# Loads of x and of the adjacency issued by ScalarE in place of SyncE, in a kernel of two graph attention layers and a multi-head attention

## The chip, the core and the metric

The kernel runs on one core of a Trainium2 chip. The metric is the device time of one execution in microseconds. SyncE (SP in the profile) has no arithmetic: here it issues all DMAs. ScalarE is ACT, VectorE DVE, GpSimd POOL, TensorE PE.

## The reference

64 independent graphs, each of 128 nodes with 256 features (float32) and an adjacency of 128 x 128 (int32). Two residual blocks are applied, each behind a layer norm and a relu:

```python
h = maximum(layernorm(x), 0)
x = x + gat(h)        # two graph attention layers
h = maximum(layernorm(x), 0)
x = x + mha(h)        # 8 heads of 32, masked by adj

def gat_layer(x, mask, W, a_src, a_dst, bias):   # H=4,F=128, elu; then H=1,F=256
    xl = (x @ W).reshape(B, N, H, F)
    e = leaky_relu(asrc[:, :, None, :] + adst[:, None, :, :], 0.2)
    attn = softmax(where(mask, e, -1e9), axis=1)
    return einsum('bsdh,bshf->bdhf', attn, xl) + bias
# mha: softmax(q k / sqrt(32), masked) v, relu, @ Wo
```

## The kernel before

All work is a software pipeline over the graphs, one graph per step. In step t, the function at lag (phase) p works on graph t - p; lags go from 0 (load of x) to 11 (store), so there are 75 steps. Each engine has a list of pairs (function, phase), written out by hand, which it runs in this order in each step. Engines meet only through semaphores: `done(eng, sem, g)` waits for a graph's result, `free(eng, sem, g, ring)` for a buffer's earlier user, and tiles have rings of 2, 4 or 8 buffers.

TensorE's list begins a step with mha's masks and scores (graph t-8) and goes on with scores of the attention layers, project_out (the output projection, L815 with attT), aggregate1, project_v and qk (L815 with h2T), aggregate2 (L929), project2 (L840) and mha_av. It ends the step with project1 (L815 with hT), which needs the transposed, normed x of graph t-3.

Matrices are multiplied in float16 halves (a high part and a remainder). The halves of h, h2, att and of the exponentials e3 are transposed by DMA: SyncE issues `dma_start_transpose` for them. SyncE's list in a step is: e3_transpose_last (phase 9, L257), att_transpose (10, L276), store of the result (11, L252), norm1_transpose (3, L263, gives hT), e3_transpose_first (8, L257), load_adj (1, L248), load_x (0, L242), norm2_transpose (6, L270, gives h2T). The first x tiles, the first adjacency and the weights are issued ahead of the steps. x_in has 8 buffers, adj_in 4. load_x waits for x1_set of graph n-8, load_adj for masks_set of graph n-4. x is first read two steps after its load (norm1_moments, VectorE), the adjacency likewise (masks, GpSimd).

ScalarE's list is relevant around mha's exponentials (phase 8, L497, four heads in each half): mha_exp_first, then elu_exp (L460), gat2_copy (L477), mha_exp_last, qk_copy (L487), gat1_exp (L448), relu2 (L482). Nothing else than ACTIVATEs is in its list. VectorE gives nmx3 (negated row maxima, L761) that the exponentials need, and gat1_recip (L752) reads the sums of gat1_exp.

Of the kernel before, what the change touches and what calls it, by code (L numbers as in the profile page):

```python
# [51 lines left out]
def wait(eng, sem, value):  # L52

    if value > 0:
        eng.wait_ge(sem, value)


def done(eng, sem, g):

    wait(eng, sem, g.n + 1)  # L60


def free(eng, sem, g, ring=2):

    wait(eng, sem, g.n + 1 - ring)
# [13 lines left out]
def gnn_kernel(nc, x, adj, W1, att_src1, att_dst1, b1, W2, att_src2, att_dst2, b2, Wq, Wk, Wv, Wo, out):  # L79
# [9 lines left out]
    with ctx:  # L89
        def sb(name, shape, dt=F32):  # L90
            return ctx.enter_context(nc.sbuf_tensor(name, shape, dt))

        def sem(name):
            return ctx.enter_context(nc.semaphore(name))
# [34 lines left out]
        x_in = sb("x_in", [128, 8, D])  # L129
        adj_in = sb("adj_in", [128, 4, N], I32)  # L130
# [72 lines left out]
        s = {n: sem(n) for n in names}  # L203
        x_here = [sem(f"x_here{i}") for i in range(8)]
        adj_here = [sem(f"adj_here{i}") for i in range(4)]
# [10 lines left out]
        def steps(body, before=None):  # L216

            def step(t):  # L220
                body([Graph(t - lag, G) for lag in range(LAGS)])

            for t in range(G + LAGS - 1):
                if before and t in before:
                    before[t]()
                step(t)

        def run(body_functions, graphs):
            for function, phase in body_functions:
                if graphs[phase].active:  # L230
                    function(graphs[phase])
# [3 lines left out]

        @block.sync
        def _(sp):
            def load_x(g):
                if g.n < 3:
                    return  # L240
                free(sp, s["x1_set"], g, 8)
                sp.dma_start(x_in[:, g.eight, :], x[g.n]).then_inc(x_here[g.eight], 16)  # L242

            def load_adj(g):
                if g.n == 0:
                    return
                free(sp, s["masks_set"], g, 4)
                sp.dma_start(adj_in[:, g.four, :], adj[g.n]).then_inc(adj_here[g.four], 16)  # L248

            def store(g):  # L250
                done(sp, s["x_out_set"], g)
                sp.dma_start(out[g.n], x_out[:, g.four, :]).then_inc(stored[g.four], 16)  # L252

            def e3_transpose(g, half, low_set):
                done(sp, s[low_set], g)
                free(sp, s["av_done"], g)
                sp.dma_start_transpose(e3T[:, g.two, half].rearrange("p s h n -> p (s h) n"),  # L257
                                       e3_split[:, g.two, half].rearrange("p s h n -> p (s h n)")).then_inc(e3T_here[2 * half + g.two], 16)

            def norm1_transpose(g):  # L260
                done(sp, s["hT_set"], g)
                free(sp, s["xl_done"], g)
                sp.dma_start_transpose(hT[:, g.two].rearrange("p s (k n) -> p (s k) n", n=N),  # L263
                                       h_split[:, g.two].rearrange("p s c -> p (s c)")).then_inc(hT_here[g.two], 16)

            def norm2_transpose(g):
                done(sp, s["h2T_set"], g)
                free(sp, s["qk_done"], g)
                free(sp, s["v_done"], g)
                sp.dma_start_transpose(h2T[:, g.two].rearrange("p s (k n) -> p (s k) n", n=N),  # L270
                                       h2_split[:, g.two].rearrange("p s c -> p (s c)")).then_inc(h2T_here[g.two], 16)

            def att_transpose(g):
                done(sp, s["attT_set"], g)
                free(sp, s["wo_done"], g)
                sp.dma_start_transpose(attT[:, g.two].rearrange("p s (k n) -> p (s k) n", n=N),  # L276
                                       att_split[:, g.two].rearrange("p s c -> p (s c)")).then_inc(attT_here[g.two], 16)

            def e3_transpose_first(g):
                e3_transpose(g, 0, "e3_low_first")  # L280

            def e3_transpose_last(g):
                e3_transpose(g, 1, "e3_low_last")

            for n in range(2):
                sp.dma_start(x_in[:, n, :], x[n]).then_inc(x_here[n], 16)
            for k in range(KD):
                sp.dma_start(w1[:, k, :, 0:HF // 2], W1[k * 128:(k + 1) * 128, :].rearrange("p (a c) -> p a c", a=2)).then_inc(s["w1_in"], 16)
            for k in range(2):
                sp.dma_start(att1[:, k, :], (att_src1, att_dst1)[k].rearrange("h f -> (h f)").partition_broadcast(128)).then_inc(s["w1_in"], 16)  # L290
            sp.dma_start(b1_all[:, :], b1.partition_broadcast(128)).then_inc(s["w1_in"], 16)
            sp.dma_start(x_in[:, 2, :], x[2]).then_inc(x_here[2], 16)
            sp.dma_start(adj_in[:, 0, :], adj[0]).then_inc(adj_here[0], 16)
            sp.dma_start(w2[:, :, 0:D], W2.rearrange("(k p) n -> p k n", p=128)).then_inc(s["w2_in"], 16)
            for k in range(2):
                sp.dma_start(att2[:, k, :], (att_src2, att_dst2)[k].rearrange("h f -> (h f)").partition_broadcast(128)).then_inc(s["w2_in"], 16)
            sp.dma_start(b2_all[:, :], b2.partition_broadcast(128)).then_inc(s["w2_in"], 16)
            for m, W in enumerate((Wq, Wk, Wv, Wo)):
                sp.dma_start(proj[:, :, m, :], W.rearrange("(k p) n -> p k n", p=128)).then_inc(s["proj_in"], 16)

            steps(lambda graphs: run([
                (e3_transpose_last, 9), (att_transpose, 10), (store, 11), (norm1_transpose, 3), (e3_transpose_first, 8),
                (load_adj, 1), (load_x, 0), (norm2_transpose, 6),
            ], graphs))

            for n in range(4):
                sp.wait_ge(stored[n], 16 * (G // 4))
# [106 lines left out]
        def _(act):  # L414
            def split_high(m):
# [2 lines left out]
                act.activation(proj_split[:, 0, :, m, :], proj[:, :, m, :], ACT.Copy, scale=scale[:, 2 + m:3 + m]).then_inc(s["split_high"], 1)  # L418
                act.activation(proj[:, :, m, :], proj[:, :, m, :], ACT.Copy, scale=scale[:, 2 + m:3 + m]).then_inc(s["w_scaled"], 1)

            def relu1(g):
                done(act, s["z_set"], g)
                wait(act, hT_here[g.two], g.dma2 - 16)
                act.activation(h_split[:, g.two, 0, :], z[:, g.two, 0, :], ACT.Relu).then_inc(s["hT_high"], 1)  # L424
# [88 lines left out]
            def att_copy(g):  # L513
# [3 lines left out]

            steps(lambda graphs: run([
                (v_copy, 9), (relu1, 3), (gat2_leaky, 6), (att_copy, 10), (abT_copy, 4), (gat1_copy, 5), (gat2_exp, 6),
                (gat1_leaky, 4), (mha_exp_first, 8), (elu_exp, 5), (gat2_copy, 6), (mha_exp_last, 8), (qk_copy, 7),  # L520
                (gat1_exp, 4), (relu2, 6),
            ], graphs), before={5: lambda: (split_high(0), split_high(1)), 6: lambda: split_high(2), 7: lambda: split_high(3)})

# [495 lines left out]
```

## Time and profile before

| | us |
|---|---|
| median of 3 runs (773.32 to 776.01) | 775.59 |
| the profiled execution | 774.69 |
| its span | 772.6 |
| TensorE busy | 716.3 |
| VectorE busy | 681.4 |
| ScalarE busy | 591.6 |
| GpSimd busy | 515.8 |

The span runs from the first to the last instruction of the profiled execution. Busy times are sums over an engine's instructions. DMA issues don't count as busy for the engine that makes them; they appear in timelines as rows of its queue (SPq is SyncE's), and their duration is that of the issue, not of the transfer. A transfer's time to landing counts from the issue's start. An idle time is put down to what ended it.

### The profile page before, as it was taken

How to read it: one execution, taken by the hardware profiler on the slowest of the kernel's cores; microseconds unless marked ns; L12 is line 12 of the kernel's file. 1: busy time of each engine (PE TensorE's matmuls, PEld its weight loads, DVE VectorE, ACT ScalarE, POOL GpSimd, SP SyncE). 2: the span in 40 equal slices, each digit the busy share in tenths (PEclk: the TensorE clock that was granted, in tenths of full speed). 3: DMA queues.
4: the chain of work that ended last, by engine and by line, in shares of the span. 5: the costliest groups of instructions: out<-in, count | busy, mean ns of one | idle time of the engine just before them, and what ended most of it. 6: DMA issues, size and time to landing. Idle time of an engine off the chain costs nothing.

```text
span 772.6 us, 26496 instructions
## 1 busy us (share of the span) xinstructions
PE 716.3 (93%) x8398; PEld 593.4 (77%) x8398; DVE 681.4 (88%) x2017; ACT 591.6 (77%) x1865; POOL 515.8 (67%) x733
## 2 busy tenths in 40 slices
PE   0389999999999999999999999999999999999973
PEld 0157788888888888888888888888888888788852
DVE  4758899999999999999999999999999989999873
ACT  0167888888888778888888788788888888788752
POOL 5456777676767676667667766676677767766551
PEclk9999999999999999999999999999999999999996
DMA  6111555666578566557766656766655666655464
GB/s 197 33 37 43 106 112 112 121 110 118 118 117 115 116 112 113 119 114 115 122 110 118 112 124 115 115 110 120 114 119 116 113 119 106 112 118 105 89 110 89
DMA packets 270423, 84.70 MB, mean 110 GB/s; under 512 B 242896, under 2 KB 269904, under 8 KB 270288
## 3 DMA queue, kind: packets, MB, share of 16 engines
q1 hardware_dynamic: 270288, 83.02, 57.8%
q8 instruction: 70, 1.15, 0.7%
q14 instruction: 65, 0.53, 0.3%
HBM read 15.86 MB, written 8.39 MB: 31 GB/s over the span
## 4 chain that ended last, share of the span: by engine, by line
PE 75%; DVE 9%; DMA 5%; issue 4%; SPq 3%; ACT 1%; POOL 1%; DVEq 0%; ACTq 0%; POOLq 0%
PE bank L815 28%; PE bank L840 11%; PE bank L986 7%; PE bank L947 6%; DMA hT<-h_split 4%; PE bank L966 3%; PE bank L929 3%; PE bank L936 3%; PE bank L866 3%; PE bank L891 2%; PE bank L889 2%; PE bank L881 2%; SPq L276 1%; DVE top L756 1%; PE bank L874 1%
## 5 line engine op out<-in xcount | busy, mean ns | idle before, releaser
L497 ACT ACTIVATE e<-bank,nmx,q_power 128x128 f32<-128x128 f32 x512 | 194.7, 481 | 5.1 <-DVE nmx L761 5.1
L372 POOL CAST e_split<-e 128x512 f16<-128x512 f32 x128 | 82.4, 643 | 118.6 <-ACT e L497 118.6
L374 POOL TENSOR_TENSOR e_split<-e,e_split 128x512 f16<-128x512 f32 x128 | 151.7, 1185 | 10.3
L840 PE MATMUL bank<-w,h1T 128*128 128x258 f32 x512 | 122.8, 382 | 0.7 <-DVE shift L599 0.7
L386 POOL TENSOR_TENSOR rstd<-var,minus_half 128x1 f32<-128x1 f32 x128 | 71.7, 560 | 66.6 <-DVE var L625 66.6
L815 PE MATMUL bank<-w_split,hT 128*128 128x260 f16 x768 | 98.2, 278 | 12.3 <-DMA hT<-h_split 11.9
L840 PEld LDWEIGHTS bank<-w,h1T 128*128 128x128 f32 x512 | 96.6, 190 | 16.6 <-DVE h1T L655 1.6
L448 ACT ACTIVATE eT<-lr,nmx 128x128 f32<-128x128 f32 x256 | 102.7, 458 | 0.8 <-DVE nmx L713 0.8
L815 PE MATMUL bank<-h2T,proj_split 128*128 128x128 f16 x1536 | 97.4, 220 | 1.6 <-DMA h2T<-h_split 1.6
L815 PEld LDWEIGHTS bank<-h2T,proj_split 128*128 128x128 f16 x1536 | 92.0, 99 | 3.7 <-DMA h2T<-h_split 2.4
L815 PEld LDWEIGHTS bank<-w_split,hT 128*128 128x128 f16 x768 | 71.1, 98 | 24.5 <-issue 7.0
L364 POOL TENSOR_TENSOR eTn<-eT,rs 128x512 f32<-128x512 f32 x64 | 67.0, 1046 | 17.9 <-DVE rs L752 17.9
L756 DVE TENSOR_REDUCE top<-bank 128x8 f32<-128x1024 f32 x64 | 77.3, 1208 | 0.3 <-PE bank L947 0.3
L424 ACT ACTIVATE h_split<-z 128x256 f16<-128x256 f32 x64 | 26.6, 416 | 65.9 <-DVE z L631 65.9
L947 PEld LDWEIGHTS bank<-qkT 32*128 32x128 f16 x1536 | 43.0, 93 | 37.7 <-issue 36.0
L986 PE MATMUL bank<-en,xl 128*128 128x128 f32 x512 | 68.3, 276 | 0.2
L448 ACT ACTIVATION_READ_ACCUMULATOR eT<-lr,nmx 128x1 f32 x256 | 65.7, 257 | 0.0
L947 PE MATMUL bank<-qkT 32*128 32x128 f16 x1536 | 64.8, 216 | 0.3 <-DVE qkT L724 0.2
L986 PEld LDWEIGHTS bank<-en,xl 128*128 128x128 f32 x512 | 62.2, 192 | 2.0 <-ACT en L455 1.3
L604 DVE SCALAR_TENSOR_TENSOR h_split<-z,h_split 128x256 f16<-128x256 f32 x128 | 61.5, 481 | 0.6 <-ACT h_split L424 0.5
L815 PE MATMUL bank<-proj_split,attT 128*128 128x256 f16 x384 | 54.3, 279 | 6.1 <-DMA attT<-att_split 6.1
L440 ACT ACTIVATE lr<-bank,ab 128x128 f32<-128x128 f32 x64 | 23.5, 368 | 43.6 <-PE bank L867 43.6
(116 smaller groups left out, 1921.7 us busy)
## 6 DMA issues: line engine op xcount, KB each, us to landing
x_in<-in_x_dram SPq DMA_DIRECT2D x64, 128.0 KB, 2.3
out_dram<-x_out SPq DMA_DIRECT2D x64, 128.0 KB, 2.0
adj_in<-in_adj_dram SPq DMA_DIRECT2D x64, 64.0 KB, 2.5
e3T<-e_split SPq DMA_TRANSPOSE x128, 3.1
hT<-h_split SPq DMA_TRANSPOSE x64, 2.4
h2T<-h_split SPq DMA_TRANSPOSE x64, 2.5
attT<-att_split SPq DMA_TRANSPOSE x64, 2.8
w<-in_L_gnn_W_dram SPq DMA_DIRECT2D x2, 256.0 KB, 3.1
```

Source lines behind the costliest of these rows:

```text
L364: pool.tensor_tensor(eTn[:, g.two, :].rearrange("p (h n) -> p h n", h=H), eT[:, g.two, :].rearrange("p (h n) -> p h n", h=H), rs[:, g.two, ...
L372: pool.tensor_copy(e3_split[:, g.two, half, 0], e).then_inc(s[high_set], 1)
L374: pool.tensor_tensor(e3_split[:, g.two, half, 1], e, e3_split[:, g.two, half, 0], ALU.subtract).then_inc(s[low_set], 1)
L386: pool.tensor_tensor(rstd[:, g.two, which:which + 1], var[:, g.two, which:which + 1], minus_half[:, :], ALU.pow).then_inc(s[rstd_set], 1)
L448: ins = act.activation(eT[:, g.two, h * N:(h + 1) * N], lr[:, g.two, h * N:(h + 1) * N], ACT.Exp, bias=nmx[:, g.two, h:h + 1], accum_out=s ...
L497: ins = act.activation(e3[:, g.two, h, :], S[:, h // 4, (h % 4) * N:(h % 4 + 1) * N], ACT.Exp, bias=nmx3[:, g.two, h:h + 1], scale=q_power ...
L604: dve.scalar_tensor_tensor(out=out_, in0=in_, scalar=0.0, in1=high_, op0=ALU.max, op1=ALU.subtract).then_inc(s[sem_], 1)
L756: dve.tensor_reduce(top3[:, g.two, :], S.rearrange("p b (h n) -> p (b h) n", h=4), AX.X, ALU.max, negate=True).then_inc(s["top3_set"], 1)
L815: ins = pe.matmul(out_, left, right, start=n == 0, stop=n == len(pairs) - 1)
L840: ins = pe.matmul(X2[:, 0:D + 2], h1T[:, g.two, k * F:(k + 1) * F], w2[:, k, :], start=k == 0, stop=k == H - 1)
L947: ins = pe.matmul(S[:, b, col * N:(col + 1) * N], qkT[r, g.two, i, h // 4, :], qkT[r, g.two, j, 2 + h // 4, :], start=False, stop=n == 2 a ...
L986: ins = pe.matmul(O1[:, h * N:(h + 1) * N], xl[:, g.two, h * F:(h + 1) * F], en[:, g.two, h * N:(h + 1) * N], start=True, stop=True)
```

## The change

load_x and load_adj move from SyncE's block to ScalarE's, with the same waits and semaphores. In ScalarE's list load_x stands behind mha_exp_first, and load_adj behind mha_exp_last. SyncE's list loses both. The loads ahead of the steps stay on SyncE.

```diff
@@ SyncE
             steps(lambda graphs: run([
                 (e3_transpose_last, 9), (att_transpose, 10), (store, 11), (norm1_transpose, 3), (e3_transpose_first, 8),
-                (load_adj, 1), (load_x, 0), (norm2_transpose, 6),
+                (norm2_transpose, 6),
             ], graphs))
@@ ScalarE
+            def load_x(g):
+                if g.n < 3:
+                    return
+                free(act, s["x1_set"], g, 8)
+                act.dma_start(x_in[:, g.eight, :], x[g.n]).then_inc(x_here[g.eight], 16)
+
+            def load_adj(g):
+                if g.n == 0:
+                    return
+                free(act, s["masks_set"], g, 4)
+                act.dma_start(adj_in[:, g.four, :], adj[g.n]).then_inc(adj_here[g.four], 16)
...
-                (gat1_leaky, 4), (mha_exp_first, 8), (elu_exp, 5), (gat2_copy, 6), (mha_exp_last, 8), (qk_copy, 7),
+                (gat1_leaky, 4), (mha_exp_first, 8), (load_x, 0), (elu_exp, 5), (gat2_copy, 6), (mha_exp_last, 8), (load_adj, 1), (qk_copy, 7),
                 (gat1_exp, 4), (relu2, 6),
```

## Rows read from the trace of the kernel before

**Rows 1.** The page: busy us (share of the span) and instructions of an engine.
```profile
PE 716.3 (93%) x8398; PEld 593.4 (77%) x8398; DVE 681.4 (88%) x2017; ACT 591.6 (77%) x1865; POOL 515.8 (67%) x733
```
**Rows 2.** Windows: stretch, then busy us (count) of PE, PEld, DVE, ACT, POOL, clock, DMA.
```profile
100.00:700.00 600.00, 596.30 (x7146) 500.63 (x7145) 562.32 (x1691) 497.96 (x1579) 423.50 (x601) 1.00 0.64 115
```
**Rows 3.** The chain of waits, its longest pieces: start us, length us, what.
```profile
93.66 2.00 PE bank L815 x30
...
203.28 2.00 PE bank L815 x30
...
214.14 2.00 PE bank L815 x30
...
709.88 2.00 PE bank L815 x30
```
**Rows 4.** Waits of the whole span: waiter, releaser, us in total, times, longest us.
```profile
DVE x L738 <- PE bank L929: 23.8, 59, 1.8
...
PE bank L815 <- DMA hT<-h_split: 11.9, 9, 7.0
```
**Rows 5.** Timeline of SyncE's queue, one undisturbed step: start us, length us, instruction.
```profile
202.87 1.19 SPq L276 DMA_TRANSPOSE attT<-att_split  x1
204.11 0.57 SPq L252 DMA_DIRECT2D out_dram<-x_out  x1
204.77 1.19 SPq L263 DMA_TRANSPOSE hT<-h_split  x1
...
207.37 0.57 SPq L248 DMA_DIRECT2D adj_in<-in_adj_dram  x1
207.99 0.44 SPq L242 DMA_DIRECT2D x_in<-in_x_dram  x1
210.46 1.20 SPq L270 DMA_TRANSPOSE h2T<-h_split  x1
```
**Rows 6.** Waits of SyncE's queue before an issue.
```profile
SPq L270 <- DVE h_split L604: 111.6, 64, 5.2
```
**Rows 7.** Timeline of ScalarE in the same step; the last row ends gat1_exp.
```profile
202.55 1.50 ACT L497 ACTIVATE e<-bank,nmx,q_power 128x128 f32<-128x128 f32 x4
...
203.93 0.70 ACT L460 ACTIVATE ex<-bank,minus_one 128x512 f32<-128x512 f32 x1
...
204.66 1.54 ACT L497 ACTIVATE e<-bank,nmx,q_power 128x128 f32<-128x128 f32 x4
...
207.96 0.25 ACT L448 ACTIVATION_READ_ACCUMULATOR eT<-lr,nmx 128x1 f32 x1
```
**Rows 8.** Timeline of VectorE: nmx3, gat1_recip, and nmx3 of the next step.
```profile
202.19 0.32 DVE L761 TENSOR_SCALAR nmx<-top,q_power 128x8 f32<-128x8 f32 x1
...
208.24 0.18 DVE L752 RECIPROCAL rs<-sm 128x4 f32<-128x4 f32 x1
...
212.93 0.32 DVE L761 TENSOR_SCALAR nmx<-top,q_power 128x8 f32<-128x8 f32 x1
```
**Rows 9.** The page's DMA issues: count, size, median us to landing.
```profile
x_in<-in_x_dram SPq DMA_DIRECT2D x64, 128.0 KB, 2.3
...
hT<-h_split SPq DMA_TRANSPOSE x64, 2.4
```
**Rows 10.** Timeline of TensorE in the same step: aggregate2 and project1.
```profile
205.11 0.65 PE L929 MATMUL bank<-xl,en 128*128 128x256 f32 x2
...
207.95 1.49 PE L815 MATMUL bank<-w_split,hT 128*128 128x260 f16 x12
```
**Rows 11.** Timeline of SyncE's queue: first and last long store, a long norm1 transpose.
```profile
138.38 1.50 SPq L252 DMA_DIRECT2D out_dram<-x_out  x1
...
248.23 2.17 SPq L263 DMA_TRANSPOSE hT<-h_split  x1
...
666.45 1.68 SPq L252 DMA_DIRECT2D out_dram<-x_out  x1
```

More of the change, by code:

```diff
@@ L237, in _ @@
         def _(sp):
[L238 to L248, printed above, removed]
             def store(g):
```

## The prediction

> **What bounds the kernel now.** I read the page's engine totals first [rows 1]: TensorE shows 716.3 us of busy time in the 772.6 us span, VectorE 681.4, ScalarE 591.6. The middle of the run is tighter than that: in the 600 us from 100 to 700, TensorE is busy 596.3, VectorE 562.3, ScalarE 498.0, at full granted clock [rows 2]. A matmul's end is modelled, so I don't take 99% as proof; the chain of waits gives a step's length. From the first to the last of its 56 middle steps (93.66 to 709.88) a step takes 11.00 us, and an undisturbed one 10.86 (203.28 to 214.14) [rows 3]. The chain in between is matmuls with no waits. So what is not TensorE's own work in the middle is (11.00 - 10.86) x 56 = 8 us. The list of waits names where it is lost: the wait for hT, SyncE's norm1 transpose, which project1 needs: 11.9 us in 9 waits, one of 7.0 among them [rows 4].
>
> **The part taken from SyncE.** Per step it loses a load of the adjacency (0.57 us) and one of x (0.44), back to back; with the gaps that is 1.06 us of a queue of 11 us [rows 5]. What stands behind them is norm2's transpose. It starts at 210.46, and the loads ended at 208.43: the queue stood empty for 2.0 us, and it waited for VectorE before all 64 of these transposes, 111.6 us in total [rows 6]. So this removal is worth nothing: norm2's transpose waits for the same h2_split as before, and what is late next is unchanged. The transposes and stores that feed project1 (att transpose at 202.87, store 204.11, norm1 transpose 204.77) come before the loads in a step; the wait of 2.0 us cuts them off from the loads of the step before. The removal can't shorten that part.
>
> **The part given to ScalarE.** 61 loads of x and 63 of the adjacency. Both free() waits are met two steps earlier (x1 of graph n-8, masks of graph n-4), so they hold nothing. The first loads may go out earlier in the ramp, before SyncE's queue of weights is through; nothing waits for them there, and I take 0. What matters is the time that the issue takes from ScalarE, and no row shows an issue on it. Bounds: nothing, if its sequencer has handed over the four exponentials and issues the load while they run (1.50 and 1.54 us [rows 7], longer than 0.44 or 0.57); the whole 1.01 us a step, if the engine stands still.
>
> What would a microsecond on ScalarE cost? The first exponentials of mha start at 202.55, as nmx3 is ready (VectorE L761 ends at 202.51 [rows 8]), then ScalarE runs without a gap through ex (203.93), the last exponentials (204.66), qk_copy and gat1_exp, which ends at 208.21 [rows 7]. VectorE's reciprocal starts at 208.24, and it runs without a gap to the next nmx3, ended at 213.25 [rows 8]. This is a loop through two engines: 213.25 - 202.51 = 10.74 us, with both loads inside its ScalarE half. Against the mean step of 11.00 it has 0.26 us to spare. Exposure below 0.26 costs nothing; all above it is paid in each of 56 steps. I take exposure near zero, since the cover is three times the issue, and keep the other end as a rival.
>
> **What the two queues do to each other.** I also have to place the moved issues on SyncE's clock. With the exponentials handed over, the x load is issued at about 202.6 to 203.1, while SyncE issues the att transpose (202.87, 1.19 us). The adjacency load comes at about 204.2 to 205, while SyncE issues the store (204.11) and norm1's transpose (204.77) [rows 5]. Today the loads stand alone. If two issues can't overlap, one of them is late: SyncE by 0 to 1.01 us a step, between independent queues and both loads in front. I take 0.57: the adjacency falls on the store or the norm1 transpose every time, while the x load is asked for before the att transpose or behind it. A gain is excluded here, since SyncE issues the same three things.
>
> The Trainium skill, page "Perfetto Trace Analysis", section "DMA Instruction — HWDGE (DVE, Sync)", speaks against this change: one descriptor generator is shared by the two issuing sequencers, and an issue's recorded time includes the wait for its lock. "DMA: Bandwidth & Descriptors", section "Issuing engines are not separate DMA queues", sees a saving of issue time alone. By the first, ScalarE's records would come out at up to one SyncE issue longer than 0.57; by independent queues, they stay at 0.43 and 0.57 and my sum is zero. No row of before has two issuers, so the trace settles neither.
>
> What is 0.57 us worth? In an undisturbed step norm1's transpose starts at 204.77 and lands 2.4 later [rows 9], at 207.2; project1 starts at 207.95 [rows 10]: 0.75 us to spare, more than 0.57. But some steps have none: 18 stores of the 56 steps, from 138.38 to 666.45, took 1.0 to 1.8 us in place of 0.57, and 2 norm1 transposes took over 2.0 [rows 11]. That extra microsecond eats the 0.75. In these 20 steps the delay reaches project1, and it returns in the step after next, since aggregate2, whose result VectorE waits for [rows 4], stands before project1 in a step (205.11 against 207.95 [rows 10]). One delay of 0.57 is thus spread over two steps, 0.29 each: 20 x 0.29 = 5.8 us.
>
> Traffic: the x load (2.3 us to landing [rows 9]) now moves beside the att transpose, the adjacency beside norm1's. A quarter microsecond on hT's landing disappears in the 0.75, and is 20 x 0.12 = 2.4 us in the disturbed steps; I leave it in the range.
>
> **Sum**, against the profiled execution's own 774.69 us (span 772.6 and 2.1 around it): 774.7 + 0 (SyncE freed) + 0 (exposure) + 5.8 = 780.5. This execution lies 0.9 below the median of the runs, 775.59; on that scale 781.4, say 781.
>
> **Rivals.**
> (a) All hidden, nothing changes. For it: ScalarE's instructions start within 0.04 us of their releaser (202.51 to 202.55), so they wait ready; the cover is 1.5 us; the freed queue time was idle. Against: the moved issues fall on the busiest stretch of SyncE. Time 775.6, give or take 3.
> (b) Faster. The mechanism: SyncE's stream is shorter, and the long issues [rows 11], which come about once a step and drift along it, fall elsewhere than on the store. Without any loss to hT the steps are 10.86: 774.7 - 8 + 0.9 = 768. For it: two thirds of the steps already run so. Against: no load stands in front of the store. It decides if the number of long stores drops below about 10.
> (c) ScalarE stands still while it issues. Exposure of all 1.01: the loop is 10.74 + 1.01 = 11.75, so 0.75 x 56 = 42 us, 817; with half of it (0.5) 11.24, 13 us, 789. It decides from an exposure of 0.26 us. For it: the loop has next to no gap. Against: the cover. The long issues are part of this: one of 1.5 to 1.9 us behind exponentials of 1.5 shows some tenths in a few steps.
>
> **How the numbers follow.** Forecast (issues contend, 776 to 792) 0.36; (a) 0.30; (b) 0.19; (c) 0.15. The forecast's low end is a third of its price, 2 us; its high end is both loads on SyncE's part every step, 0.5 x 20 + (1.01 - 0.75)/2 x 36 = 15 us. About 0.5% (3.9 us) is what a measurement can tell from no change. Slower: all of (c) and nine tenths of the forecast, 0.47. Same: the rest of the forecast and nearly all of (a), 0.33. Faster: 0.20. The range for 8 in 10 goes down to (b), 768, and up through the forecast into the half-exposed (c), 800. The forecast's own range is 776 to 792.
>
> **What the new profile would show.** Right: loads at ScalarE's queue with issues clearly over 0.57 us, or SyncE's store and norm1 transpose longer or later by about half a microsecond; ScalarE's gap between exponentials and ex under 0.1 us; TensorE's waits for hT grown by about 6 us; SyncE's wait before norm2's transpose up by about 1 us a step, to some 170 us. Wrong: load issues at 0.43 and 0.57 with no gap behind them (then (a)); fewer long stores and a mean step near 10.86 ((b)); VectorE waiting for eT or for ex by more than 0.3 us a step, and a step of over 11.3 us ((c)). The prediction fails altogether if a ramp step's loads arrive late and norm1_moments waits for x.

## The result, and the profile after

The changed kernel takes 776.91 us (median of 22 runs, 775.29 to 781.02), the kernel before in the same comparison 774.48 (22 runs). The ratio is 1.0039, with a 95% interval of 1.0027 to 1.0051: slower by 0.4%, some 2.4 to 3 us. The direction is that of the forecast; the forecast's 781 asked for more than twice as much.

The profiled execution took 775.29 us, its span is 773.5. It is the quickest of the 22, so its span, 0.9 us over that of before, does not show the whole loss. First the page of the changed kernel, the issues with their median us to landing.

```profile
out_dram<-x_out SPq DMA_DIRECT2D x64, 128.0 KB, 2.6
x_in<-in_x_dram ACTq DMA_DIRECT2D x61, 128.0 KB, 2.5
adj_in<-in_adj_dram ACTq DMA_DIRECT2D x63, 64.0 KB, 2.8
...
hT<-h_split SPq DMA_TRANSPOSE x64, 2.5
...
attT<-att_split SPq DMA_TRANSPOSE x64, 3.5
```

The same two rows on the page of the kernel before, for the store and the att transpose:

```profile
out_dram<-x_out SPq DMA_DIRECT2D x64, 128.0 KB, 2.0
...
attT<-att_split SPq DMA_TRANSPOSE x64, 2.8
```

The DMAs that SyncE issues beside the moved loads land later, the att transpose by 0.7 us and the store by 0.6; hT by 0.1 in the median against [rows 9]. Now the waits of the changed kernel, of TensorE and of SyncE's queue, to be read against [rows 4] and [rows 6] (us in total, times, longest us):

```profile
PE bank L815 <- DMA hT<-h_split: 13.1, 10, 7.0
```
```profile
SPq L258 <- DVE h_split L604: 186.8, 64, 6.3
```

SyncE now waits 75 us longer before norm2's transpose, 1.17 a step: the freed 1.06 us turned into waiting. TensorE waits 1.2 us longer for hT. The issues themselves, in the timeline of ACT, its queue and SyncE's in one step (start us, length us, instruction):

```profile
203.29 0.33 ACTq L413 DMA_DIRECT2D x_in<-in_x_dram  x1
203.34 1.50 ACT L497 ACTIVATE e<-bank,nmx,q_power 128x128 f32<-128x128 f32 x4
...
203.60 1.19 SPq L264 DMA_TRANSPOSE attT<-att_split  x1
...
204.38 0.33 ACTq L419 DMA_DIRECT2D adj_in<-in_adj_dram  x1
...
204.70 0.71 ACT L460 ACTIVATE ex<-bank,minus_one 128x512 f32<-128x512 f32 x1
...
204.84 0.57 SPq L240 DMA_DIRECT2D out_dram<-x_out  x1
...
205.43 1.55 ACT L497 ACTIVATE e<-bank,nmx,q_power 128x128 f32<-128x128 f32 x4
```

The reader is to see three things. The four exponentials still take 1.50 us and ex still follows within their tail, so nothing of an issue is exposed (no ScalarE time stands still for it). The adjacency is issued at 204.38, 1.05 us before the exponentials that stand ahead of it in the list start: the sequencer runs ahead. And this issue lies wholly inside SyncE's issue of the att transpose (203.60 to 204.79); the transpose has its usual length, and the load's 0.33 us is that of an undisturbed issue there, as the run with the late loads shows below.

### The profile page after: what moved, and what is told of

It is laid out like the page before. It is cut to its first block, busy times and chain, and to the rows that moved or that the text cites. A ratio compares the mean times of both kernels' runs of the same rounds, so it can differ in the third digit from the quotient of the medians.

```text
span 773.5 us, 26496 instructions
## 1 busy us (share of the span) xinstructions
PE 714.1 (92%) x8398; PEld 592.0 (77%) x8398; DVE 681.2 (88%) x2017; ACT 590.8 (76%) x1865; POOL 515.0 (67%) x733
## 4 chain that ended last, share of the span: by engine, by line
PE 72%; DVE 10%; DMA 6%; issue 4%; SPq 3%; ACT 3%; POOL 1%; DVEq 0%; POOLq 0%; ACTq 0%
PE bank L815 27%; PE bank L840 10%; PE bank L986 6%; PE bank L947 6%; DMA hT<-h_split 4%; PE bank L966 3%; PE bank L929 3%; PE bank L936 3%; PE bank L866 3%; DVE top L756 2%; PE bank L891 1%; PE bank L889 1%; PE bank L881 1%; SPq L264 1%; ACT e L497 1%
```

## The experiments

Ratios are to the kernel before as it was timed in the same comparison. There were three: its median was 774.06 us beside the two runs on the start and the first two reorderings, 775.00 beside the halves, the late loads and the doubled load, and 773.83 beside the small loads and the last two reorderings. The changed kernel itself was timed in none of the three, so it is compared with them through its own ratio, 1.0039. The edits are shown shortened.

**The start.** In the profiles the second graph's project1 starts at 38.45 us after against 37.58 before (the first graph's at 26.85 against 26.00). The first three loads now go out among the weights; they were put back on SyncE, and in the mirror image they alone were moved.

```diff
+ SyncE:   (load_adj, 1), (load_x, 0), (norm2_transpose, 6)   # x: only g.n == 3; adj: only g.n in (1, 2)
- ScalarE: if g.n < 3: return        # load_x
+ ScalarE: if g.n <= 3: return       # load_x;  load_adj: if g.n <= 2: return
```

> The changed kernel, but the three loads that go out before the weights have landed (adjacency of graphs 1 and 2, x of graph 3) stay on SyncE at their old place; from x of graph 4 and adjacency of graph 3 on ScalarE issues all. Theory A (the loss is in the start: in the changed kernel these three loads share the DMA engines with the weights, and the first project1 starts 0.87 us later): the first project1 is back at 37.6 us, and the time comes down by 0.9 us from the changed kernel, to about 775.4, ratio to before 1.001 to 1.003. Theory B (the loss is in the middle, where the loads now move beside the att and norm1 transposes and the stores): the start comes back, but the time stays 1.5 us or more over before, ratio 1.002 to 1.005. Theory C (contention of issues, the step of the prediction): no difference to the changed kernel, ratio 1.004. Both A and B can hold: the part of the start is 0.0011 of the ratio.

Measured: 776.54 us, ratio 1.0037 (1.0022 to 1.0053). With the start undone, the loss is still there. The loss is in the middle, as theory B has it. The time alone can't part B from theory C (contention of issues), which expected 1.004; the lengths of the issues and the small loads further down do. This profile, of an execution of 778.19 us, also shows the loss where the page of the changed kernel hardly did: TensorE's wait for hT has gone from 11.9 us in 9 waits to

```profile
PE bank L827 <- DMA hT<-h_split: 16.6, 15, 7.0
```

```diff
  # mirror image: ScalarE only x of g.n == 3 and adj of g.n in (1, 2); SyncE x of g.n > 3, adj of g.n > 2
```

> The mirror image: ScalarE issues only the three early loads (adjacency of graphs 1 and 2, x of graph 3), SyncE all others as before. Theory A: the first project1 about 0.9 us later than in the kernel before (38.4 to 38.5), ratio 1.001 to 1.0015 if the loss of the start is kept to the end, with the middle steps as before (10.99 us each). Theory B alone: ratio 1.000. Theory C: ratio 1.000, since in the middle nothing contends.

Measured: 774.04 us, ratio 1.0001 (0.9987 to 1.0015). Theory A is out as the account of the loss: undoing the start leaves a ratio of at least 1.0022, and moving the start alone gives none that can be measured. The interval would still allow A's own 0.001, but not its mechanism: with the three early loads on ScalarE, the second graph's project1 starts at 36.87 us in this profile, earlier than in the one of before. The 0.87 us was a difference between two executions.

**One half at a time**, early loads left on SyncE.

```diff
+ SyncE:   load_adj (all), load_x (g.n == 3)
+ ScalarE: (mha_exp_first, 8), (load_x, 0)    # g.n > 3
```

> One half of the change: ScalarE issues the loads of x (graph 4 on), behind mha_exp_first; all adjacency loads and x of graph 3 stay on SyncE. So far the whole change without its early loads costs 0.37% (2.5 us of the median), in the middle. Theory T (traffic: the load's transfer now runs beside the att transpose, the store and the norm1 transpose, whose landings went from 2.8 to 3.3, 2.0 to 2.5, and 2.4 to 2.6 us): the cost goes by bytes and place, x is 128 KB of 192, ratio 1.0015 to 1.004, att transpose landing over 3.1. Theory Q (the second queue itself costs, wherever its transfers run): half of it, ratio 1.001 to 1.003, the landings of SyncE's DMAs as with the whole change only if it is the queue. Theory N (noise of the phase between steps and long issues): 0.999 to 1.001.

Measured: 774.21 us, ratio 0.9990 (0.9973 to 1.0007).

```diff
+ SyncE:   load_x (all), load_adj (g.n in (1, 2))
+ ScalarE: (mha_exp_last, 8), (load_adj, 1)   # g.n > 2
```

> The other half: ScalarE issues the adjacency loads (graph 3 on) behind mha_exp_last, in fact some 0.4 us before SyncE issues the store; all loads of x stay on SyncE. Theory T: 64 KB of 192, but in 512 B packets and nearer to hT: ratio 1.0005 to 1.002; att transpose landing about 2.9, hT landing up by 0.1. If T holds with the place before the bytes, this half carries most: 1.002 to 1.004. Theory Q: about as much as the x half, 1.001 to 1.003. Theory N: 0.999 to 1.001.

Measured: 773.45 us, ratio 0.9988 (0.9972 to 1.0004). Each half alone costs nothing that can be measured; both together cost 0.37%. The cost is not a sum over the loads, as theory T and theory Q had it in these expectations: even the upper ends of the two intervals add up to 0.11%. Both values lie in the range of theory N, by which the loss comes from how the long issues fall on the steps. These two runs don't exclude N; the small loads below speak against it.

**The same loads later**, where SyncE's queue had stood empty.

```diff
- (mha_exp_first, 8), (load_x, 0), ... (mha_exp_last, 8), (load_adj, 1), (qk_copy, 7),
- (gat1_exp, 4), (relu2, 6),
+ (mha_exp_first, 8), ... (mha_exp_last, 8), (qk_copy, 7),
+ (gat1_exp, 4), (relu2, 6), (load_adj, 1), (load_x, 0),
```

> The changed kernel with both loads later in ScalarE's list, behind relu2, so that they are issued where SyncE issued them before (the queue between e3_transpose_first and norm2_transpose), but from ScalarE's queue. Theory T (place of the traffic): the loss goes, ratio 0.999 to 1.0015, landing of the att transpose back to 2.8, of the store to 2.0. Theory Q (a second queue costs): ratio stays 1.003 to 1.005. An exposure on ScalarE would show here: relu1 and relu2 wait for VectorE anyway (0.66 and 0.39 us a step), so at most 0.1 us a step.

Measured: 776.71 us, ratio 1.0019 (1.0003 to 1.0036). The page gives 2.7 us for the att transpose's landing and 2.0 for the store's, back at the level of before, as T said; but the time lies between the two theories and its interval touches both. Between T and Q it decides nothing, since this place has a cost of its own. From 100 to 700 us the list of waits has two rows that the kernel before doesn't have:

```profile
ACT vv L492 <- issue: 39.8, 54, 1.8
...
PE bank L874 <- DVE ab_split L667: 2.5, 7, 0.5
```

Behind relu2, which waits for VectorE, the adjacency is issued only as relu2 itself starts (210.78 us against 210.77 in one step). The x load follows it, and the next copy (v_copy, L492) waits for both issues, 0.7 us a step. Most of it is time in which ScalarE waited for VectorE before anyway. But 9 of the x issues took up to 1.74 us in place of 0.45, and each of TensorE's 7 waits at L874 follows one of them (1.27 to 1.74 us). Here the issues are exposed, and the 2.5 us are enough for the 0.19%. That they are all of it is not shown.

**More of the suspected cost.** 56 more loads of 128 KB behind the same exponentials.

```diff
                 act.dma_start(x_in[:, g.eight, :], x[g.n]).then_inc(x_here[g.eight], 16)
+                if g.n >= 8:
+                    wait(act, spare_here[g.eight], g.dma8 - 32)
+                    act.dma_start(spare[:, g.eight, :], x[g.n]).then_inc(spare_here[g.eight], 16)
```

> The changed kernel, and behind each load of x from graph 8 on a second load of the same 128 KB into a spare tile that nothing reads (56 more). Theory T: the suspected cost doubles or more, 4.5 to 8 us over before, ratio 1.006 to 1.010, landing of the att transpose near 4, of the store near 3. Exposure on ScalarE (a third issue of 0.33 us behind exponentials of 1.5) should stay nil: the gap between the exponentials and ex does not grow; if it does, the loop through ScalarE and VectorE of 10.74 us passes 10.86 and the steps get longer by it, ratio above 1.02. If traffic costs nothing and the loss has another cause: ratio 1.003 to 1.005, as the changed kernel.

Measured: 798.66 us, ratio 1.0323 (1.0281 to 1.0365), three times what theory T had at the most, and in the range that the expectation gave to exposure on ScalarE. Its page and its waits (line numbers moved by 2 to 5):

```profile
out_dram<-x_out SPq DMA_DIRECT2D x64, 128.0 KB, 3.7
...
hT<-h_split SPq DMA_TRANSPOSE x64, 3.5
...
attT<-att_split SPq DMA_TRANSPOSE x64, 4.1
```
```profile
PE bank L820 <- DMA hT<-h_split: 30.8, 26, 7.0
```

hT lands 1.0 us later than in the changed kernel, more than the spare of 0.75 us, so that TensorE waits for it 26 times, against 10. These waits have grown by 18.9 us over before, of 23.7 lost. That is why this dose costs so much more than the first. ScalarE's timeline is the control: with three issues a step, ex follows the exponentials without a gap. From 100 to 700 us there is one exception, of 0.2 us, so the loss is not exposure.

```profile
299.50 1.16 ACT L502 ACTIVATE e<-bank,nmx,q_power 128x128 f32<-128x128 f32 x3
...
300.52 0.71 ACT L465 ACTIVATE ex<-bank,minus_one 128x512 f32<-128x512 f32 x1
```

**Fewer bytes, the same issues**, once on each queue.

```diff
+                part = slice(0, 128 if g.n < 8 else 16)      # adj: g.n < 4
-                act.dma_start(x_in[:, g.eight, :], x[g.n]).then_inc(x_here[g.eight], 16)
+                act.dma_start(x_in[part, g.eight, :], x[g.n][part, :]).then_inc(x_here[g.eight], 16)
```

> The changed kernel with small loads: from x of graph 8 and the adjacency of graph 4 on, only 16 of the 128 nodes' rows are moved (16 KB and 8 KB in place of 128 and 64); so most of x and adj that the graphs are computed from is that of earlier graphs. Number, place and waits of the DMAs are those of the changed kernel. Theory T (transfer): the whole loss goes, the landings of att transpose and store fall below 2.9 and 2.1 us, ratio 0.994 to 0.999. Theory Q (a second queue, or SyncE's shorter stream, costs without bytes): ratio stays 1.002 to 1.005.

Measured: 773.68 us, ratio 0.9997 (0.9980 to 1.0014). The page's landings are 2.8 us for the att transpose and 2.1 for the store.

> The kernel before with the same small loads on SyncE, in their old place; the same part of x and adj is left stale. Tells what the loads' bytes cost where they were. They moved in SyncE's empty stretch before norm2's transpose, so nearly nothing: ratio 0.997 to 1.000. With the small loads on ScalarE: if both give the same time within 0.15%, the queue and the place of the issue are free and the loss of the change is the bytes beside the path; if this one is 0.3% faster, theory Q.

Measured: 774.33 us, ratio 1.0001 (0.9983 to 1.0020). With an eighth of the bytes the two placings are the same within the error of some 0.2%: the second queue, the place of the issue and SyncE's shorter list cost nothing that can be measured, and less than the 0.27% that the change costs at the least. The loss of the change goes with the bytes. Both expectations' ranges (0.994 to 0.999 and 0.997 to 1.000) were missed narrowly: taking the bytes away removes the loss, but gains nothing over before.

**The DMA that is on the path.** The store stands between the att transpose and norm1's, whose landing project1 needs.

```diff
- (att_transpose, 10), (store, 11), (norm1_transpose, 3),
+ (att_transpose, 10), (norm1_transpose, 3), (store, 11),
```

> The kernel before, with SyncE's norm1 transpose ahead of the store in a step. The store (0.57 us, in one of three steps 1.0 to 1.8) leaves the way to hT, whose wait is what TensorE loses in the middle. If the path att transpose, store, norm1 transpose sets the lost 8 us of the middle: mean step from 11.00 towards 10.86, time 767 to 771, ratio 0.990 to 0.995. If the long issues only move on to the next DMA (the one that now stands between att transpose and hT's landing is one less, so the chance to be hit is smaller, but not nil): ratio 0.994 to 0.998. If another wait (att transpose behind att_split of VectorE, or VectorE and ScalarE's loop of 10.74) takes over: ratio 0.998 to 1.002.

Measured: 769.17 us, ratio 0.9933 (0.9917 to 0.9949). The wait for hT is now 8.9 us in 3 waits, 7.0 of it the one at the start:

```profile
PE bank L815 <- DMA hT<-h_split: 8.9, 3, 7.0
```

The same, by moving the store to ScalarE instead:

```diff
- SyncE:   (store, 11)
+ ScalarE: (mha_exp_last, 8), (store, 11), (qk_copy, 7)
```

> The kernel before, with the stores issued by ScalarE behind mha_exp_last and the loads left on SyncE: the same edit as the change, but made to the DMA that stands on SyncE's path to hT. If an issue on ScalarE is free (0.33 us behind exponentials), and SyncE's path sets the lost 8 us: ratio 0.990 to 0.996. The store waits for x_out_set, which VectorE gives about when ex starts, and it stops ScalarE's sequencer: if that wait or the store's long issues show on ScalarE, VectorE's waits for eT or ex grow and the ratio is 0.998 to 1.01. If the traffic, not the issue, delays hT, the ratio is 0.997 to 1.001.

Measured: 771.17 us, ratio 0.9959 (0.9945 to 0.9973). The edit of the case, made to the DMA that is on the path, gains; the mere reordering gained more in these runs and needs no second queue.

The changed kernel with norm1's transpose ahead of the store:

> The changed kernel with norm1's transpose ahead of the store on SyncE, which in the kernel before gave a ratio of 0.9933. The store's 0.66 us leaves the path to hT, so hT has some 1.4 us to spare in an undisturbed step instead of 0.75. Theory T (the change costs only what its traffic adds to hT's landing beyond the spare): with the larger spare the loss of 0.37% shrinks to 0.1% or nothing: ratio 0.993 to 0.995. If the cost has nothing to do with hT's spare: 0.9933 + 0.0038 = 0.997.

Measured: 772.93 us, ratio 0.9987 (0.9974 to 1.0001). The expectation failed: the loss from the change did not shrink to 0.1% but is 0.9987/0.9933, 0.5%, which the intervals don't tell from the 0.4% of before. TensorE's waits for hT are 11.0 us in 8, against 8.9 in 3 without the change. The landings of hT from 100 to 700 us (min, median, max) point to the reason, first here, then in the reordered kernel without the change:

```profile
DMA to landing us min/median/max: 2.4/3.1/4.8
```
```profile
DMA to landing us min/median/max: 2.4/2.7/4.3
```

Norm1's transpose, moved up, now runs nearer the loads' transfers, lands 0.4 us later in the median and eats a part of the spare it won. Whether that is the whole 0.5% no run tested.

Last, both DMAs put behind norm1's transpose, with the loads on SyncE:

```diff
- (att_transpose, 10), (store, 11), (norm1_transpose, 3),
+ (norm1_transpose, 3), (att_transpose, 10), (store, 11),
```

> The kernel before, with SyncE's order norm1 transpose, att transpose, store: both DMAs that stood before norm1's transpose go behind it. hT_set comes 0.33 us after attT_set from VectorE, so norm1's transpose starts 0.9 us earlier than with the store alone moved, and the att transpose 1.6 us later; attT is read in the next step's project_out, over 8 us later. If hT's wait is still what is lost in the middle (2.5 us of excess over 10.86 in 56 steps is left with the store moved): ratio 0.989 to 0.993. If what is left is something else: 0.992 to 0.995.

Measured: 767.67 us, ratio 0.9925 (0.9909 to 0.9941). It is faster than both kernels of the case. Its intervals overlap with those of the first reordering, so of the two neither is shown to be the better. From 100 to 700 us its TensorE is busy for all 600.00 us, against 596.30 in [rows 2]:

```profile
100.00:700.00 600.00, 600.00 (x7228) 504.83 (x7228) 564.85 (x1710) 501.90 (x1597) 430.10 (x607) 1.00 0.62 116
```

## Why the prediction was wrong

- **What bounds the kernel, and 8 us lost in the middle to hT**: right. The two reorderings on SyncE took 5 to 6 us of it.
- **SyncE freed, worth nothing**: right. The wait grew to 186.8 us; some 170 were forecast.
- **Exposure on ScalarE zero**: right for these places in the list, and the rival (c) is out here: even three issues a step leave one gap of 0.2 us in the middle of the run. It is not so everywhere: behind relu2 the same issues held ScalarE up by 0.7 us a step. What I had not seen is how far ahead the sequencer runs. I placed the x load at 202.6 to 203.1 and the adjacency at 204.2 to 205 on the clock of before; the second in fact comes before ex, inside the att transpose's issue, not at the store.
- **Issues contend, 0.57 us x 20 steps, 5.8 us**: this is the step that failed. The issues on ScalarE took 0.334 us in the median of 107, none above 0.69, and SyncE's kept their length. Of the 54 adjacency issues from 100 to 700 us, 46 lie wholly inside an issue of SyncE. The term is zero. A shared wait can't be hidden in the 0.334 us either: in the run with the late loads, 50 of the 54 adjacency issues ran while SyncE issued nothing, and took 0.334 us as well. Here are the source views of the adjacency load and of the att transpose in that stretch, min/median/max in ns:

```profile
L419 ACTq DMA_DIRECT2D adj_in<-in_adj_dram x54: 334/334/691, 105.8 to 689.8; - x54
```
```profile
L264 SPq DMA_TRANSPOSE attT<-att_split x54: 1188/1189/2022, 105.1 to 689.1; - x54
```

  The rule of the Trainium skill (page "Perfetto Trace Analysis", section "DMA Instruction — HWDGE (DVE, Sync)"), by which two sequencers share one descriptor generator and the recorded issue holds the wait for its lock, is not borne out by these rows: no such wait is in them. (The page names DVE and Sync as the two; here they are ScalarE and SyncE.) That the transfers of two issuers interleave and a second one saves only issue time (the Trainium skill, page "DMA: Bandwidth & Descriptors", section "Issuing engines are not separate DMA queues") agrees with the landings: SyncE's att transpose and store landed 0.7 and 0.6 us later beside ScalarE's loads.
- **Traffic, a quarter microsecond on hT in the disturbed steps, 2.4 us, left out of the sum and kept for the range**: this was the term to take. The loss measured is 2.4 to 3 us; it goes with the bytes and grows with them. The size on hT was below the quarter microsecond: counted from the end of its issue, so that a long issue doesn't enter, its mean landing from 100 to 700 us went from 1.32 us to 1.41 after, and to 1.53 with the start undone. So that the price fits is partly luck. The same shows in the halves: worked out the same way, each half of the change would have had a share of it, and neither shows one.
- **The spare of 0.75 us** explains why a delay is free up to a point and dear beyond it; the dose of 56 loads, with hT 1.0 us later, agrees. In the change hT's median landing moved by only 0.1 us; the difference is in the late ones. From 100 to 700 us, norm1 transposes that landed more than 1.5 us after their issue had ended were 6 of 54 before, 7 and 6 of 55 and 54 with the small loads on ScalarE and on SyncE, 9 after and 16 of 54 with the start undone, and 43 of 52 with the doubled load. But the halves had 14 (x) and 11 (adjacency), at no measured loss. So that each half fits in the spare and both do not is not shown, and why the cost is not a sum stays open.
- **Rival (a)**, nothing changes, 775.6 give or take 3: its time holds, and its account of the issues was the right one. It had no term for the transfers, which are the loss.
- **Rival (b)**: no. After, 12 stores and 10 norm1 transposes were long; with only the three early loads moved it was 13 and 10 at an unchanged time. So the place of the long issues shifts between profiles with no change of the time, and a count from one profile, as mine of 20, is a weak base for a term.
- **The range**: by its own two prices, 2 and 15 us on 775.6, the forecast spans 778 to 791; the 776 to 792 written down is wider at both ends without a reason. The measured 776.9 lies below what the terms give.

Open are why the two halves together cost what neither costs alone, how much of the loss hangs on the place of the traffic rather than on its queue (the late loads can't say, since they were exposed on ScalarE), and what makes an issue long.

## What to carry to other kernels

A queue with idle time gains nothing from losing a DMA that stands in front of the idle time; look for what stands between the last producer and the transfer that is waited for, and put that behind it. A DMA moved to another engine is issued when that engine's sequencer reaches it. Behind instructions that are handed over early that was 1.05 us before they ran, and it cost ScalarE nothing; behind one that waits for another engine it came late and held up the next instruction by 0.7 us. Its bytes then share the DMA engines with whatever is in flight there. If that is a transfer with little to spare, a free issue costs time.

## What the runs showed of the hardware

The length of a load's issue went by the engine and by what stood right before it, not by which of the two loads it was. On SyncE an issue of x took 0.43 us right behind that of the adjacency, and 0.57 alone (the run with the adjacency on ScalarE); the adjacency took 0.57. On ScalarE both took 0.33 us alone, and the second of two in a row 0.45 (x in the run with the late loads, the spare in the doubled load). A load issued by ScalarE while SyncE issued a transpose lengthened neither: 0.334 us and 1.19 us in the median, as without the other.

In every second step or more an issue takes about a microsecond more, whichever it is. From 100 to 700 us, 37 of SyncE's issues before and 28 after took over 0.4 us more than the median of their kind. By the packet records of the traces every one of them coincides with one of the instruction packets of q8 (16 KB each, 70 in the run), as do the 9 long issues of x on ScalarE with the late loads; of the other SyncE issues, 36 of 398 before and 22 of 298 after do. The packets follow each other every 10.5 us where a step takes 11.0, which fits the drift of the long issues along the step. No run varied the packets, so the link is a coincidence in time and not shown to be the cause.
